# Two graph layers on one TensorE stream: a new order for the blocks, the first chain and the last outputs

## The reference

```python
# layer 0
h = relu(adj @ x @ gcn_w + gcn_b);  h = layernorm(h) * ln_g + ln_b
xc, z = split(h @ w_in)                          # 256 + 256 columns
u = silu(causal_conv4(xc) + conv_b)
dt_r, B, C = split(u @ w_xp)                     # 8 + 16 + 16 columns
dt = softplus(dt_r @ w_dt + b_dt)
hst[t] = exp(dt[t] * A) * hst[t-1] + dt[t] * B[t] * u[t]      # 256 x 16 states, a scan over 4096 rows
y = (hst @ C + u * D_skip) * silu(z)
x1 = layernorm(x + y @ w_out)
# layer 1
out1 = mlp3((2 + eps1) * (adj @ x1), W1, b1)
out2 = mlp3((2 + eps2) * (adj @ x2), W2, b2)
out = layernorm(x1 + concat(out1, out2) @ Wm.T + bm)
```

## Time and profile before

| | |
|---|---|
| median of 3 runs | 832.26 us (831.99 to 838.22) |
| the profiled execution's own time | 836.52 us |
| its span, first to last instruction | 834.7 us |
| mean granted clock of PE | 0.987 |
| PE busy | 808.9 us, 97% |
| POOL busy | 662.5 us, 79% |
| DVE busy | 606.0 us, 73% |
| ACT busy | 380.1 us, 46% |
| DMA | 226.56 MB, mean 271 GB/s |

### The profile page before, as it was taken

One profiled execution on the slowest core, in us unless ns is written; L12 is line 12 of the kernel. 1 busy time (PEld: TensorE's weight loads), 2 busy tenths in 40 slices (PEclk: granted clock), 3 DMA queues, 4 the chain that ended last, 5 costly groups with the idle time before them and its releaser, 6 DMA issues.

```text
span 834.7 us, 7328 instructions
## 1 busy us (share of the span) xinstructions
PE 808.9 (97%) x2074; PEld 366.1 (44%) x2074; DVE 606.0 (73%) x805; ACT 380.1 (46%) x615; POOL 662.5 (79%) x322
## 2 busy tenths in 40 slices
PE   6999989999999999999999999999989999999995
PEld 2444434444444444444444444444434444444453
DVE  0020998789878978997799889888987897752134
ACT  0043575347534753575357535753565362301234
POOL 2002999999999999999999999999988999800046
PEclk9999998999999999999999999999999999999998
DMA  8978865865766788767886778799999999968602
GB/s 342 397 295 278 268 211 190 297 210 197 266 249 192 245 284 297 260 245 235 272 286 222 245 266 298 236 367 357 355 326 335 340 355 383 397 254 278 225 25 77
DMA packets 63101, 226.56 MB, mean 271 GB/s; under 512 B 7362, under 2 KB 8276, under 8 KB 44628
## 3 DMA queue, kind: packets, MB, share of 16 engines
q1 hardware_dynamic: 24084, 155.28, 50.2%
q10 hardware_dynamic: 38976, 70.80, 26.6%
HBM read 223.43 MB, written 2.62 MB: 271 GB/s over the span
## 4 chain that ended last, share of the span: by engine, by line
PE 88%; DVE 5%; DMA 2%; POOL 1%; issue 1%; ACT 1%; ACTq 1%; POOLq 0%; DVEq 0%
PE p_x L484 48%; PE p_x L505 18%; PE p_two L505 8%; DVE p_h L907 3%; PE p_m L576 2%; PE p_m L592 2%; DVE prod L916 1%; PE p_dA L663 1%; DMA x_s<-x_tiles 1%; POOL mb L410 1%; PE p_two L566 1%; PE p_m L596 1%; PE p_m L588 1%; PE p_m L530 1%; PE p_m L559 1%
## 5 line engine op out<-in xcount | busy, mean ns | idle before, releaser
L484 PE MATMUL p_x<-ring,x_s 128*128 128x512 f32 x1024 | 459.9, 600 | 7.8 <-DMA x_s<-x_tiles 7.8
L1097 POOL TENSOR_TENSOR y<-y,prod 128x1024 f32<-128x1024 f32 x127 | 298.8, 2353 | 18.4 <-DVE prod L916 17.6
L484 PEld LDWEIGHTS p_x<-ring,x_s 128*128 128x128 f32 x1024 | 195.2, 192 | 259.6 <-issue 249.1
L1088 POOL TENSOR_TENSOR bh<-spread,dtu 128x1024 f32<-128x1024 f32 x128 | 301.5, 2356 | 1.8 <-DMA spread<-bc_rows 1.8
L907 DVE TENSOR_TENSOR_SCAN p_h<-p_dA,state,bh 128x512 f32<-128x512 f32 x224 | 276.2, 1279 | 32.1 <-ACT p_dA L673 17.9
L673 ACT ACTIVATE p_dA<-dt,A 128x512 f32<-128x512 f32 x256 | 171.8, 687 | 148.6 <-DVE p_h L907 141.8
L505 PE MATMUL p_x<-ring,x 128*128 128x512 f32 x352 | 158.0, 598 | 0.8 <-issue 0.8
L916 DVE TENSOR_TENSOR prod<-p_h,spread_C 128x1024 f32<-128x1024 f32 x128 | 155.4, 1214 | 0.2 <-issue 0.2
L505 PEld LDWEIGHTS p_x<-ring,x 128*128 128x128 f32 x352 | 66.3, 191 | 84.0 <-issue 84.0
L410 POOL TENSOR_SCALAR mb<-prod,mv,rstd 128x128 f32<-128x128 f32 x30 | 23.4, 793 | 76.9 <-ACT rstd L894 76.2
L932 DVE TENSOR_TENSOR acc<-p_x,acc 128x512 f32<-128x512 f32 x30 | 20.7, 689 | 72.9 <-PE p_x L505 72.9
(11 more groups left out here) (122 smaller groups left out, 578.5 us busy)
## 6 DMA issues: line engine op xcount, KB each, us to landing
ring<-adj_blocks SPq DMA_DIRECT2D x143, 1024.0 KB, 7.0
spread<-bc_rows ACTq DMA_DIRECT2D x128, 256.0 KB, 4.8
spread_C<-bc_rows ACTq DMA_DIRECT2D x128, 256.0 KB, 5.6
x_s<-x_tiles SPq DMA_DIRECT2D x8, 256.0 KB, 7.3
x_s<-x_tiles ACTq DMA_DIRECT2D x7, 256.0 KB, 17.0
out_tiles<-mb SPq DMA_DIRECT2D x7, 256.0 KB, 2.0
pack<-pack_w ACTq DMA_DIRECT2D x1, 1026.5 KB, 23.9
ring<-adj_blocks SPq DMA_DIRECT2D x4, 256.0 KB, 4.3
```

Of the source, the lines that this page charges most:

```text
L484: last = pe.matmul(bank[:, :], tiles[:, j, :], ring[:, i % RING, jt, :], start=j == 0, stop=j == N // P - 1)
L1088: pool.tensor_tensor(bh[:, i % 3, :, :], both(spread[:, i % SLOTS, :]), dtu[:, c % 2, :, :], ALU.mult).then_inc(s_bmul, 1)
L1097: pool.tensor_tensor(y[:, c % 2, :, :], y[:, c % 2, :, :], prod[:, i % 2, :, :], ALU.add).then_inc(s_acc, 1)
```

## The change

- The order of the blocks is written out, chunk by chunk. A block may now serve x2 and x1 together ("x2", "x1": `DOUBLE`), which 23 loads do, all in rows 0, 1, 5, 6 and 7. Rows 5, 6 and 7 of x, which shared their loads with x2, have loads of their own now. There are 145 loads in all, where there were 144. The chunks hold 80, 80, 84, 80, 80, 88, 84 and 76 block matmuls (before: 80 each), in 10, 10, 17, 17, 16, 17, 15 and 14 loads (before: 10, 10, 12, 12, 12, 16, 20 and 20). Thirteen blocks are left behind chunk 7 (before: 16). Sums of the second pass are listed in `SUMS`, 30 of them (before: 40), over two to six blocks each.
- `FILL` becomes 0, 1, 3, 7, 3 and 18. The four tiny matmuls for the biases (L609) move from ahead of the gcn step to behind it.
- ACT issues the first two spread rows right behind the "rows" step, ahead of softplus, and takes row 1 of x in unit 0 of chunk 0 and no longer ahead of y_init.
- In chunk 0 `origin` is 4 (before: 3). PE does its steps half a unit before those of the other chunks.
- From chunk 1 on, dt comes half a unit later, and mlp0 to mlp3 stand two half units apart, at 24, 26, 28 and 30 (before: 24 to 27).
- Before the first block PE runs three matmuls of 128x256 on zeros. The x tiles 1 to 3 come in one DMA (rows of 1536 bytes) where there were three (rows of 512).
- The outputs are staged in four buffers (dtu's memory, free by then); DVE normalises row 6 and the last half row, POOL the rest.

```diff
+STAGES = 4
+WARM, WARM_W = 3, 256
...
-FILL = {"gcn": 3, "cen": 3, "var": 5, "in_x": 13, "x_proj": 5, "dt": 3}
+ONE, X, X2, X1, DOUBLE = ("x", "x2"), ("x",), ("x2",), ("x1",), ("x2", "x1")
+FILL = {"gcn": 0, "cen": 1, "var": 3, "in_x": 7, "x_proj": 3, "dt": 18}
+CHUNK_BLOCKS = [
+    [(("x2", "x"), 2, 0)] + row(ONE, 2, ALL[1:]) + row(ONE, 3, ALL[:2]),
+    row(ONE, 3, ALL[2:]) + row(ONE, 4, ALL[:4]),
+    row(ONE, 4, ALL[4:]) + row(X, 5, ALL[:6]) + row(X1, 2, (0, 1)) + row(X, 5, (6, 7)) + row(X1, 3, (0, 1))
+    + row(X, 6, (0,)),
+    row(X, 6, (1,)) + row(X1, 4, (0, 1)) + mixed(row(X, 6, ALL[2:]), row(X2, 0, ALL[3:])) + row(DOUBLE, 0, ALL[:3]),
+    row(X, 7, (0,)) + row(DOUBLE, 1, (0, 1)) + mixed(row(X, 7, ALL[1:]), row(X2, 1, ALL[4:])) + row(DOUBLE, 1, (2, 3)),
+    row(DOUBLE, 5, ALL[:4]) + row(X2, 5, (5, 6)) + row(DOUBLE, 5, (4,)) + row(X2, 5, (7,))
+    + row(X1, 2, (2, 3, 4)) + row(X1, 4, (2, 3, 4)) + row(X1, 3, (2, 3, 4)),
...
+X2_ROWS = (2, 3, 4, 0, 1, 5, 6, 7)
+SUMS = [("two", 2, (0, 1)), ("two", 3, (0, 1)),
...
 def origin(c):
-    return 3 if c == 0 else 4
+    return 4
...
-        return [(c - 1, (24, 25, 26, 27))]
-    return [(6, (6, 8, 10, 12)), (7, (26, 27, 28, 29))]
+        return [(c - 1, (24, 26, 28, 30))]
+    return [(6, (6, 8, 10, 12)), (7, (24, 26, 28, 30))]
...
-        at = (6, 8, 10, 12, 16, 18) if c == 0 else tuple(2 * origin(c) + q for q in (-1, 1, 2, 4, 9, 11))
+        at = tuple(2 * origin(c) + q - (c == 0) for q in (-1, 1, 2, 4, 9, 12))
...
+            pe.wait_ge(s_idle, 1)
+            for _ in range(WARM):
+                pe.matmul(p_m[:, 0:WARM_W], sq[:, 0:P], sq[:, 0:WARM_W], start=True, stop=True)
...
+            def first(i, part, jt):
...
+                if opens:
...
+                    wait(pe, s_taken, taken)
...
+            def second(i, jt, chunk, unit):
...
+                        pe.wait_ge(s_zcopy, G * (chunk + 1))
+                        if unit > origin(chunk) and chunk + 1 < NC:
+                            pe.wait_ge(s_dt, G * (chunk + 1) + 1)
...
             def take_x2(n):
                 q = X2_ROWS.index(n)
-                act.wait_ge(s_blk_used, last_block(n, 1) + 1)
+                act.wait_ge(s_blk_used, LAST_OF["x2", n] + 1)
...
-            for jt in range(JT):
-                act.dma_start(x_s[:, jt, :], x_d[0, :, jt]).then_inc(s_tile[jt], 16)
+            act.dma_start(x_s[:, 0, :], x_d[0, :, 0]).then_inc(s_tile[0], 16)
+            act.dma_start(x_s[:, 1:JT, :], x_d[0, :, 1:JT]).then_inc(s_tile[1], 16)
...
-                if name == "softplus":
-                    take_x(1)
+                if name == "rows":
+                    for i in range(AHEAD):
+                        spread_row(i)
...
+                    if c == 0 and unit == 0:
+                        take_x(1)
...
-            normalise(dve, NC - 1, range(JT // 2, JT), NC, s_fin_last)
+            normalise(dve, NC - 2, range(JT), NC - 2, s_fin_dve)
+            normalise(dve, NC - 1, range(JT // 2, JT), NC, s_fin_dve)
```

More of the change, by code:

```diff
@@ L70 @@
[L70 to L92, removed]
@@ L95, with row, mixed @@
-AFTER_BLOCKS = [("two", 6, k) for k in range(NBLK)]
-AFTER = len(AFTER_BLOCKS)
-TAIL_BLOCKS = [("two", NC - 1, k) for k in range(NBLK)]
+def row(what, n, columns):
+    return [(what, n, m) for m in columns]
+ALL = range(NBLK)
+ONE, X, X2, X1, DOUBLE = ("x", "x2"), ("x",), ("x2",), ("x1",), ("x2", "x1")
+def mixed(*lists):
+    return [b for q in range(max(len(p) for p in lists)) for p in lists for b in p[q:q + 1]]
+RAMP = row(X, 0, ALL)
+FILL_BLOCKS = row(X, 1, ALL)
+FILL = {"gcn": 0, "cen": 1, "var": 3, "in_x": 7, "x_proj": 3, "dt": 18}
@@ L100 @@
 FIRST = []
-for _c in range(NC):
+for _blocks in CHUNK_BLOCKS:
     FIRST.append(len(LOADS))
-    LOADS = LOADS + chunk_blocks(_c)
+    LOADS = LOADS + _blocks
 AFTER_AT = len(LOADS)
@@ L463, in _ @@
+            for q in range(STAGES):
+                sp_.wait_ge(s_out[q], 16 * (NC // STAGES + (q == k % STAGES)))
         @block.tensor
         def _(pe):
-            def one(i, lo, hi):
-                kind, n, k = LOADS[i]
+            def first(i, part, jt):
+                _, n, m = LOADS[i]
+                bank, tiles, s_taken, taken = ((p_x, x_s, s_ax, n) if part == "x" else
+                                               (p_x2, x2_s, s_ax2, X2_ROWS.index(n)))
+                opens = jt == 0 and i == FIRST_OF[part, n]
+                closes = jt == JT - 1 and i == LAST_OF[part, n]
+                if opens:
+                    wait(pe, s_taken, taken)
+                if part == "x2" and jt == 0 and i < FIRST[1]:
+                    pe.wait_ge(s_x2s[m], 16)
+                return pe.matmul(bank[:, :], tiles[:, JT * m + jt, :], ring[:, i % RING, jt, :],
+                                 start=opens, stop=closes)
@@ L467, in one, with block_part @@
+            def block_part(i, lo, hi, chunk=NC - 1, unit=S):
+                steps = block_steps(LOADS[i])
                 if lo == 0 and i:
                     pe.wait_ge(*filled(i))
[L469 to L487 removed]
@@ L617, in _ @@
                 if name == "gcn":
+                    for q in range(2 * G):
+                        last = pe.matmul(p_h[:, 1, q:q + 1], w_in[:, P * q:P * (q + 1)], w("ln_b"),
+                                         start=True, stop=True)
+                    last.then_inc(s_bxzp, 1)
                     pe.wait_ge(s_cen_w, 1)
```

269 lines of the change are left out of this document (121 added, 148 removed), and 4 rows, old and new, of the table SUMS.

## The result

| | before | after |
|---|---|---|
| median of the runs | 832.4 us (831.99 to 838.22, 4 runs) | 822.65 us (822.47 to 822.95, 4 runs) |
| ratio | | 0.9866, 95% interval 0.9829 to 0.9903 |
| the profiled execution's own time, span | 836.52, 834.7 us | 822.56, 820.8 us |
| mean granted clock of PE | 0.987 | 0.998 |

The change makes the kernel 1.3% faster. Predicted were 819.1 us for the median and 823.3 us for a profiled execution: the first was 3.6 us off, within its range, the second 0.7.

A forecast was written before the change was run, and what follows sets the result against it. PE bounds the kernel at 97% of the span, POOL next at 79%. Terms -8.7 - 4.1 - 0.7 - 0.8 - 2.0 + 1.5 + 0.7 + 0.9 = -13.2 take the 832.3 us median to 819.1, range 814.5 to 827.

The forecast's parts named there:

- Chunk 0, the largest term: Chunk 0: the shorter first chain gives DVE and ACT enough lead to remove PE's waits and half clock, -8.7 us.
- Rival (b): Chunk 0: ACT and DVE stand still at PE's z step, the lead is gone, waits stay; 828 us, chance 0.08.
- Chunk 6: Chunk 6: the later dt removes the 2.29 us wait before dt and the half clock behind it, -4.1 us.
- The new waits: Two new PE waits: p_two sum behind dt in chunk 2, +0.7; row 5's start behind x2's row 1, +0.9 us.
- The loads: 145 loads for 144, chunk 3 rising to 325 GB/s: costs nothing, with POOL's spare time as cover.
- Rival (c): Whole scan: DVE's new waits at softplus and mlp3 stop POOL, which becomes the pace; slower, 847 us, chance 0.07.
- POOL idle over 3 us in chunk 3: Sign in the changed profile, also for chunks 1 or 4, said to prove (a) or Rival (c).
- (a): Chunks: one or two new waits over 2 us bring half clock, half given back; 823 to 827 us, chance 0.19.
- The end: After the last matmul: DVE takes row 6, so POOL needs six tiles and DVE ends last, -2.0 us.
- The start: Ramp: fewer packets bring data sooner and zeros raise the clock for the first block, -0.7 us, between +1 and -3.
- 1.3 us for the x tile: Ramp: with fewer packets the second block's x tile should be there about 1.3 us sooner.
- the median of the runs, 832.3, becomes **819.1 us: Last step: the sum of -13.2 us, from the profiled execution, is applied to the median of the runs.

The follow-up runs named there:

- after_waits_mended: Changed kernel with chunk 2's dt earlier, chunk 5's first block x1 half first, row 6's MLP steps at 7, 10, 12, 14, tiny matmuls ahead of gcn: 819.0 us.
- after_old_start: Changed kernel without the three matmuls on zeros and with three x tile DMAs again: 822.27 us.
- run 2: Not a label of any run: the words belong to "a run 2 us or more above their lowest", where 2 us is a time difference.

## Why the prediction was right, and where it was off

**Chunk 0, the largest term, held.** The shorter chain took all waits and the half clock out of chunk 0: -8.7 predicted, -8.75 in the pair. Done alone it gave -7.6 at the median, where chunk 0, the chain and the tiny matmuls (-8.7 + 1.5) sum to -7.2. Rival (b), that the lead is lost at z and the waits stay, falls. The lead of DVE and ACT was enough, though smaller than thought: the first scan is 14.7 us behind dt and not 12.3. Softplus starts 4.0 us later behind dt than before (62.89 - 57.67 against 72.56 - 71.40), and the earlier spreads give back only the 1.8 us for which POOL's first bh had waited for its row:

```profile
62.89 0.60 ACT L772 ACTIVATE dt<-p_two 128x512 f32<-128x512 f32 x1 [5.33 <-issue]
```

```profile
81.35 4.74 POOL L1088 TENSOR_TENSOR bh<-spread,dtu 128x1024 f32<-128x1024 f32 x2 [1.78 <-DMA spread<-bc_rows]
```

The first of these rows is of the changed kernel, the second of the one before.

**Chunk 6 held in size, its cause only in part.** The later dt is worth 4.1 us in the kernel before, as predicted. In the changed kernel it is worth nothing: without it no dt waits, and the stream is 1.2 us shorter. There the new block order and the spaced MLP steps had already moved what made ACT late, and which of them did isn't settled.

**The new waits.** Chunk 2 (0.7 predicted, 0.70 in the timeline) and the start of row 5 (0.9, 0.94) came as computed, and both vanished with the edits aimed at them. The prediction's step "Two new waits for PE remain" failed in its count. It checked the banks and the copies, but for the MLP steps only what DVE does, and not what stands ahead of the copy on ACT: the x1 steps, which wait for DVE. That is 1.6 us. The mends of after_waits_mended together gave back 3.65 at the median and 4.2 in the stream, against 0.70 + 0.94 + 1.58 us of the three waits and 0.78 idle ahead of gcn, 4.0 together.

**The loads** cost nothing, as predicted: at 322 GB/s in chunk 3 PE's and POOL's idle times stay below what matters. Rival (c), POOL as the pace, falls too. POOL was idle 4.9 us in chunk 2, 4.3 in chunk 3, and 8.8 in chunk 5. In chunks 3 and 5 PE stood still for 0.01 us at most, and its 0.5 in chunk 2 were for DVE. The prediction had said that POOL idle over 3 us in chunk 3 would prove (a) or (c). It was, and neither came: that sign was wrong, because idle time of POOL costs nothing as long as PE doesn't wait for what POOL makes.

**The end** held: -2.0 predicted, -2.8 from PE's last matmul to the end, 2.3 by the experiment. The row says that DVE's six tiles ran at 1.60/6 = 0.27 us each while POOL ran its last two. POOL's two took 0.79 and 0.85, where it takes 0.79 alone. The Trainium skill (GPSIMD Engine Reference, Key points) says that POOL contends for its SBUF interfaces with VectorE's instructions that run in a 2-port mode or read two inputs from SBUF. Taken to hold for these tiles it would have left a gain of 0.5; the trace shows 0.05 us on one tile.

**The start** was mis-sized, and its reason was wrong. The pair shows -2.0, but the experiment shows nothing for the edit at the median. The -2.0 are 1.7 of half clock that one execution of before had in its ramp and two others hadn't, and 0.3 of an earlier second block (12.93 against 13.21). No row stood behind the prediction's 1.3 us for the x tile. The tile did come sooner (landed at 8.8 us, before at 13.2), but the block itself came later (12.8, before 11.8), and PE waits for that one now (`[2.12 <-DMA ring<-adj_blocks]`), and the zeros didn't have the clock up for the first block: its first matmul still took 2.07 us for two records.

**The median.** The step that is weak is the last: "the median of the runs, 832.3, becomes **819.1 us**". It takes the whole -13.2 of one profiled execution from the median of three runs. But the profiled execution was 4.3 us above that median, and so held losses that a median run didn't. Against its own session the change gained 9.8 us at the median (832.4 to 822.65). The sum predicted 13.2, and the 1.6 for mlp1 unforeseen leaves 11.6. The other 1.8 us are put down to the base.

What makes the kernel before slower in one run than in another is known only in part. Each run also lists its mean clock. Over the 49 further runs of before (median 833.9, 831.29 to 837.51) the 13 at a clock of 0.989 have a median of 835.0 us, the 12 at 0.993 and above 832.4. So less half clock goes with less time. But the 16 runs at 0.991 alone lie between 831.3 and 837.4, so something that the mean clock doesn't tell moves them too; the three profiles show one such thing, the ramp's end, which moved by 2.7 us. The changed kernel's four runs, at 0.997 to 0.999, lie within 0.5 us. That the change narrows the spread because it takes waits away fits this, but isn't shown: after_old_start, with the same waits in its stream, spread over 4.3 us in six runs. The six changed kernels with the old start all had a run 2 us or more above their lowest, of the five with the new start only one. So the steadier ramp seems to have a part in it.

From the 833.9 of all further runs the sum would have given 833.9 - 13.2 + 1.6 = 822.3, close to the measured 822.65. That base was picked afterwards and from other sessions, so the closeness is partly luck.

**One rule of the rivals.** Rival (a) says "A wait over 2 us brings half clock". The waits of 2.11 and 2.12 us in the last section brought none, so it is not a rule.

## What to carry to other kernels

When one engine is the pace, list its idle times from the trace, price each with its clock behind it, and move the steps that end late. Here three small parts (the first chain, the spacing of the steps, the end) gained as much without the new order of blocks as with it, and that order brought waits of its own. When a step is moved, go through the queue of the engine that answers it, and not only through the bank that it needs: what stood behind a wait there (x1's steps ahead of mlp1's copy, row 1's copy behind a decay) is the next wait. And a gain read from one profiled execution belongs to that execution: set it against a base whose losses are the same, or take two more profiles of the kernel before and see which losses come back.
